# Relative scores of a small-head attention added onto an open group of TensorE as fp32 transpositions instead of products with the identity

## The reference, cut to what matters

```python
q = hidden_states @ Wq.T + bq
k = hidden_states @ Wk.T + bk
v = hidden_states @ Wv.T + bv
...
score1 = jnp.einsum('bhqd,bhkd->bhqk', qh, kh)
rel_k = _rel_embeds(rel_k_emb, T, T)
s2 = jnp.einsum('bhqd,qkd->qbhk', qh, rel_k)
s2 = s2.reshape(T, H, B, T).transpose(2, 1, 0, 3)
scores = (score1 + s2) / scaling
attn = jax.nn.softmax(scores, axis=-1)
w1 = jnp.einsum('bhqk,bhkd->bhqd', attn, vh)
rel_v = _rel_embeds(rel_v_emb, T, T)
se = attn.reshape(B * H, T, T).transpose(1, 0, 2)
w2 = jnp.einsum('qnk,qkd->qnd', se, rel_v)
...
out = (w1 + w2).transpose(0, 2, 1, 3).reshape(B, T, E)
return out @ Wo.T + bo
```

## Time and profile before

| | |
|---|---|
| median of 3 runs | 1376.2 us (1375.03 to 1377.79) |
| profiled execution: span from first to last instruction | 1375.6 us |
| its own time | given only as that span; the median of the runs is 0.6 us above it |
| PE busy | 1217.7 us, 89% of the span, 9574 instructions |
| DVE busy | 701.2 us, 51% |
| ACT busy | 534.1 us, 39% |
| POOL busy | 441.7 us, 32% |
| mean granted clock of TensorE | 0.920 of full speed |
| L2 attention, first to last instruction | about 776.6 to 943.8 us |
| its loop over score groups | about 828 to 903 us |

### The profile page before, as it was taken

One profiled execution on the slowest core, in us unless ns is written; L12 is line 12 of the kernel. 1 busy time (PEld: TensorE's weight loads), 2 busy tenths in 40 slices (PEclk: granted clock), 3 DMA queues, 4 the chain that ended last, 5 costly groups with the idle time before them and its releaser, 6 DMA issues. The chain is left out here.

```text
span 1375.6 us, 24268 instructions
## 1 busy us (share of the span) xinstructions
PE 1217.7 (89%) x9574; PEld 879.5 (64%) x9574; DVE 701.2 (51%) x2149; ACT 534.1 (39%) x1186; POOL 441.7 (32%) x521
## 2 busy tenths in 40 slices
PE   6999898999868785998798789998989999978997
PEld 5868676788723352665466487795657775556676
DVE  5555543444478335674576466626842125754512
ACT  5534242444355432354345372213433323343232
POOL 7959320000155415672675240003000002031314
PEclk9999999999956587999899999999989998988899
DMA  5000312322091000000000000000020100000412
GB/s 163 1 4 1 142 58 75 95 62 63 21 298 42 1 1 33 1 1 0 1 1 1 9 1 1 1 4 2 1 84 31 47 16 14 1 4 1 140 48 51
DMA packets 51632, 52.42 MB, mean 38 GB/s; under 512 B 19552, under 2 KB 42336, under 8 KB 50496
## 3 DMA queue, kind: packets, MB, share of 16 engines
q1 hardware_dynamic: 50496, 48.77, 11.3%
q0 software_dynamic: 1024, 2.10, 0.7%
HBM read 43.65 MB, written 7.21 MB: 37 GB/s over the span
## 5 line engine op out<-in xcount | busy, mean ns | idle before, releaser
L625 ACT ACTIVATE scratch<-bank 128x512 f32<-128x512 f32 x96 | 52.4, 594 | 87.8 <-PE bank L524 87.8
L584 DVE TENSOR_REDUCE scratch<-bank 128x4 f32<-128x512 f32 x96 | 63.1, 686 | 32.7 <-PE bank L2506 19.5
L447 POOL TENSOR_TENSOR ln_rstd<-ln_ve,ln_half 128x4 f32<-128x4 f32 x28 | 28.7, 1025 | 157.7 <-DVE ln_ve L426 157.6
L2770 POOL TENSOR_TENSOR scratch<-scratch 128x16 f32<-128x16 f32 x16 | 51.7, 3230 | 50.1 <-DVE scratch L3112 50.1
L1126 ACT ACTIVATE scratch<-bank 128x512 f32<-128x512 f32 x64 | 38.2, 597 | 67.8 <-PE bank L1085 67.8
L1095 PEld LDWEIGHTS bank<-scratch 128*128 128x128 f32 x512 | 59.5, 192 | 7.2 <-issue 7.2
L1145 DVE SCALAR_TENSOR_TENSOR x_res<-bank,scratch,x_res 128x128 f32<-128x128 f32 x64 | 18.0, 344 | 88.0 <-PE bank L1095 88.0
L590 DVE TENSOR_TENSOR scratch<-bank,scratch 128x512 f32<-128x512 f32 x96 | 61.4, 681 | 0.0
L1085 PE MATMUL bank<-xnT,scratch 128*128 128x512 f32 x128 | 60.1, 615 | 0.0
L1095 PE MATMUL bank<-scratch 128*128 128x128 f32 x512 | 59.6, 275 | 0.0
L524 PEld LDWEIGHTS bank<-ident,scratch 128*128 128x128 f32 x384 | 42.5, 143 | 22.6 <-DVE scratch L590 15.9
(11 more groups left out here) (570 smaller groups left out, 3087.3 us busy)
## 6 DMA issues: line engine op xcount, KB each, us to landing
scratch<-conv_kernels SPq DMA_DIRECT2D x8, 1024.0 KB, 11.1
scratch<-e_l_ffn_w SPq DMA_DIRECT2D x20, 256.0 KB, 2.9
scratch<-e_l_ffn_w SPq DMA_DIRECT2D x4, 1024.0 KB, 14.5
values<-scratch SPq DMA_DIRECT2D x8, 512.0 KB, 2.6
scratch<-values SPq DMA_DIRECT2D x8, 512.0 KB, 4.3
weights<-w_l_ffn SPq DMA_DIRECT2D x1, 3698.0 KB, 11.5
scratch<-e_l_ffn_w SPq DMA_DIRECT2D x4, 768.0 KB, 9.5
weights<-w_l_attn SPq DMA_DIRECT2D x1, 2560.5 KB, 8.6
```

The source lines that it names most:

```text
L584: self.nc.vector.tensor_reduce(self.top[:, n % 4, :], self.by_head(self.core.ps[n % 4][:, :]), AX_X, ALU.max, negate=True).then_inc(self.t ...
L625: self.nc.scalar.activation(self.prob_of(n), self.by_head(self.core.ps[4 + n % 2][:, :]), ACT.Exp, scale=scale) \
L2770: nc.gpsimd.tensor_tensor(rn, ss, power, ALU.pow).then_inc(rooted.sem, rooted.up())
```

## The change

The argument `is_transpose=True` is added to the matmul of `relative`. The operands, the order of the instructions, the semaphores, the banks and the flags start and stop are as before. `pe_turn` and `pe_back` issue the same kind of instruction by way of `nc.tensor.transpose`, not onto open groups.

```diff
@@ -2504,7 +2504,7 @@
                 for n in (2 * p, 2 * p + 1):
                     for i in range(4):
                         s = nc.tensor.matmul(ps[n % 4][:, i * P:(i + 1) * P], sm.prob_of(n)[:, i, :],
-                                             core.ident[:, :], start=False, stop=(i == 3))
+                                             core.ident[:, :], start=False, stop=(i == 3), is_transpose=True)
                     s.then_inc(sm.scores.sem, sm.scores.up())
```

## The result

The changed kernel takes 1357.0 us in the median of 7 runs (1353.19 to 1366.63) and the kernel before, run beside it, 1375.03 us (7 runs). The ratio is 0.9889, with a 95% interval from 0.9865 to 0.9913: 15.3 us less, between 12 and 18.6. The two medians themselves are 18.0 us apart; what follows goes by the ratio and its interval.

What follows compares the result with a forecast made beforehand. TensorE's (PE's) list was taken as the bound: 14.9 us saved, less waits of 0.45 and 0.1, gives 14.35; the 1375.6 us span becomes 1361.25, plus 0.6 for the median, 1361.8 us. Range 1357.8 to 1366.0.

Steps and rivals of the forecast that it cites:

- What bounds the kernel: In the stretch the diff touches, TensorE's own list is the path: PE busy 69.00 of 69 us, VectorE waiting for it.
- The price of a transposition: Eight transpositions in relative take 0.95 us in the loop instead of 1.88, and 1.02 instead of 1.98 ahead of it.
- The bound of no gain: Dear end of the price: eight adding transpositions in relative cost as much as today's products, 1.88 us, gain nothing.
- The waits: New PE waits: 0.45 us for the shift at step 2, 0.1 us at the turning at the loop's end.
- DVE's cover: In the loop VectorE keeps pace: about 3.0 us of work per step against PE's 3.7, with 1.7 us in hand.
- the falling clock: Transpositions in the loop don't keep TensorE's clock up; loop's 60 us become 114, whole 1416 us; chance 6%.
- no effect: Transpositions onto an open group in L2506 run in two passes like products, 256 records, 1376.2 us; chance 4%.
- the late VectorE: VectorE becomes the loop's bound, at 4.2 us a step; gain only 7 us, 1369 us; chance 7%.
- the cheaper transposition: Transpositions in relative pack closer than 0.1075 us, say 0.08; gain 18 us and more, 1358 us; chance 4%.
- The step that missed: Added 1.5 us to both ends of the spread for clock falls at the beginning of later parts.

## Why the prediction was right, and what it missed

**What bounds the kernel** held: PE's list, in every step. Half the change gave half the gain, twice the transpositions took it away.

**The price of a transposition** was taken as 0.95 us for eight in the loop and came out at 0.97; ahead of the loop 1.02 as booked (825.31 to 826.33). The bound of no gain is excluded: adding costs a transposition nothing.

**The waits**: 0.45 us booked at step 2, 0.28 measured (PE got there later than reckoned: the second relative group was put at 0.95 us there, though its own price ahead of the loop was 1.02); at the loop's end 0.1 booked, none measured. 14 x (1.88 - 0.97) + 2 x (1.98 - 1.02) - 0.28 = 14.4 us, and the loop shrank by 14.4 in each of the four profiles of the changed kernel.

**DVE's cover**: there was more of it than I gave, 2.7 us of work in a step rather than 3.0, against 3.7 of PE's.

**The rivals**: the falling clock, no effect, the late VectorE and the cheaper transposition are all excluded in the loop. The first was argued from a wrong count: a step of the changed kernel has 16 or 20 transpositions, 2.1 of 3.7 us, not 24 and 2.6; the long run of 256 settles it whatever the share. It has a grain of truth in another place: an idle PE of 2 us, which a shorter list can cause, can be followed by a fall, as in the kernel without the relative scores.

**The step that missed** is the last one, from the loop to the median: I gave the clock's falls in other parts 1.5 us and called that the distance between the runs shown; those three lay 2.8 us apart. The seven runs of the changed kernel spread over 13 us and those of the kernel before over 8. The first two profiles differ by 10 us outside the changed part, and so the median of 1357.0 came to lie below my range. That the first ratio agrees with the forecast to 1 us (1360.9 and 1361.8) is in part luck: the four comparisons of the change have ratios of 0.9889, 0.9907, 0.9927 and 0.9904, the mean being 0.9907 or 12.8 us, which would make it 1363.4. The loop alone would give 0.9895. That value lies in three of the four intervals and 0.0009 outside the third. Whether the 1.6 us between the two are chance or a small loss elsewhere stays open; no profile shows such a loss.

## What to carry to other kernels

An fp32 product with the identity that only turns a tile and adds it onto an open group can be a transposition: half the TensorE time (0.110 us in place of 0.225 for 128x128), same operands, flags and waits. Such a gain is whole where TensorE's list is contiguous; look for the first place where the list then has to wait, and at the granted clock behind it (an idle 2.05 us was followed by 13 us at the lower level here, and a filler prevented it). Size a filler by the rows of its own kind, in records, and end it before the awaited data arrive.

## What the runs showed of the hardware that I had not expected

- Transpositions alone held the upper clock level for 28 us, 256 in a row at a granted clock of 1.00.
- An idle PE of 2.05 us was followed by 13 us at the lower level, and a filler in its place by none. But 2.19 us of idle time in another part were followed by no fall.
- Products with 32 rows: those of two steps, eight records on all four groups of rows, took 1.14 us in one piece, while those of one step, four records on two of the groups, take 1.13. Issued together, the second pair is nearly free.
- The same instructions behind the changed part took 431.8 us in one execution and 425.1 in another, with PE 8.2 us less busy at 0.96 in place of 0.93. On another chip they took 441.2 and 438.0 us at 0.93, so the clock is not all that differs.
